# Two experts per token by sorting into blocks, in place of all four with a gate

## What is computed

```python
x = x + conv(_gn(x))                        # spike attention, 8 heads, values rounded to 0..4
t = _to_tokens(x)
t = t + attention(_ln_t(t))                 # causal, 6 heads of 32
t = t + ffn(_ln_t(t))
...
scores = jnp.einsum('bsd,de->bse', x, gate_w) + gate_b          # 4 experts
probs = jax.nn.softmax(scores, axis=-1)
topk_vals, topk_idx = jax.lax.top_k(probs, TOP_K)               # TOP_K = 2
mask = jnp.sum(jax.nn.one_hot(topk_idx, NUM_EXPERTS), axis=-2)
masked = probs * mask / (jnp.sum(probs * mask, axis=-1, keepdims=True) + 1e-09)
h = gelu(jnp.einsum('bsd,edh->ebsh', x, w1) + b1)               # 192 -> 768
y = jnp.einsum('ebsh,ehd->ebsd', h, w2) + b2                    # 768 -> 192
out = jnp.einsum('bse,ebsd->bsd', masked, y)
```

## Time and profile before

| | us |
|---|---|
| median of 3 runs | 1736.04 (1730.72 to 1737.88) |
| the profiled execution | 1726.64 |
| its span, first to last instruction | 1724.8 |
| PE busy | 1581.2 |
| DVE busy | 1211.1 |
| ACT busy | 932.3 |
| POOL busy | 234.4 |

### The profile page before, as it was taken

How to read it: one execution, slowest core, us unless ns; L and a number is a source line. 1 busy time by engine, 2 the same in 40 slices (tenths; PEclk the granted TensorE clock), 3 DMA queues, 4 the chain that set the end, 5 groups by cost and what they waited for, 6 DMA issues and landing times.

```text
span 1724.8 us, 32985 instructions
## 1 busy us (share of the span) xinstructions
PE 1581.2 (92%) x13264; PEld 1018.6 (59%) x13264; DVE 1211.1 (70%) x2544; ACT 932.3 (54%) x1378; POOL 234.4 (14%) x296
## 2 busy tenths in 40 slices
PE   1579999899999999999999999999999999999998
PEld 0334576556765566655765557654666556765666
DVE  6776875857867676767758587676776777686743
ACT  2315655366544765456553665537654566536664
POOL 3021112011020112001030110201111010301100
PEclk9668999999999999999999999999999999999999
DMA  4221002010020001010020100201001100200000
GB/s 128 97 55 38 1 1 65 1 48 1 1 65 29 20 1 46 20 48 1 2 65 1 47 2 1 65 1 47 1 22 45 47 2 2 64 2 11 1 10 10
DMA packets 25102, 48.19 MB, mean 28 GB/s; under 512 B 7411, under 2 KB 16819, under 8 KB 23573
## 3 DMA queue, kind: packets, MB, share of 16 engines
q1 hardware_dynamic: 15840, 28.63, 6.1%
q0 software_dynamic: 6144, 9.45, 2.3%
q10 hardware_dynamic: 2966, 8.01, 1.3%
HBM read 20.70 MB, written 6.29 MB: 16 GB/s over the span
## 4 chain that ended last, share of the span: by engine, by line
PE 64%; DVE 25%; ACT 5%; issue 3%; DMA 1%; POOL 1%; SPq 0%; DVEq 0%; ACTq 0%
PE ps L429 20%; PE ps L707 16%; PE ps L654 8%; DVE mx L1157 7%; PE ps L464 5%; PE ps L588 4%; DVE acc L1313 3%; DVE room L1329 3%; PE ps L508 2%; DVE u L1027 2%; PE ps L436 1%; DVE norm_stats L998 1%; PE ps L495 1%; ACT room L870 1%; DVE gn_st L1040 1%
## 5 line engine op out<-in xcount | busy, mean ns | idle before, releaser
L870 ACT ACTIVATE room<-ps,b_sb 128x512 f32<-128x512 f32 x384 | 263.2, 686 | 461.9 <-PE ps L429 460.7
L707 PE MATMUL ps<-wout_h,room 128*128 128x192 f16 x3072 | 462.4, 247 | 5.4 <-DVE acc L1313 5.4
L1329 DVE SCALAR_TENSOR_TENSOR room<-room 128x512 f16<-128x512 f32 x384 | 263.6, 690 | 177.8 <-ACT room L876 172.8
L707 PE MATMUL ps<-wout_l,room 128*128 128x192 f16 x1536 | 379.4, 247 | 0.0
L707 PEld LDWEIGHTS ps<-wout_h,room 128*128 128x128 f16 x3072 | 287.8, 98 | 46.0 <-DVE acc L1313 11.8
L848 ACT ACTIVATE room<-ps 128x1024 f32<-128x1024 f32 (+3 forms) x288 | 225.4, 809 | 143.1 <-PE ps L468 90.8
L1157 DVE TENSOR_REDUCE mx<-ps 128x2 f32<-128x1024 f32 (+3 forms) x288 | 266.3, 953 | 40.4 <-PE ps L592 19.9
L876 ACT ACTIVATE room<-room 128x512 f16<-128x512 f32 x384 | 241.9, 630 | 34.3 <-PE ps L707 0.7
L654 PE MATMUL ps<-room,v 128*64 128x512 f32 (+3 forms) x1152 | 232.6, 488 | 0.0
L588 PE MATMUL ps<-qk 96*128 96x512 f16 (+3 forms) x576 | 160.6, 352 | 37.6 <-DVE mx L1157 28.2
L464 PE MATMUL ps<-qk 98*64 98x512 f16 (+3 forms) x1152 | 157.2, 333 | 11.7 <-DVE mx L1157 7.8
(11 more groups left out here) (210 smaller groups left out, 2382.3 us busy)
## 6 DMA issues: line engine op xcount, KB each, us to landing
xc<-x_ch SPq DMA_DIRECT2D x8, 768.0 KB, 6.0
qk<-qk_all SPq DMA_DIRECT2D x96, 64.0 KB, 2.5
qk<-qk_all POOLq DMA_DIRECT2D x96, 64.0 KB, 2.5
out<-acc ACTq DMA_DIRECT2D x16, 384.0 KB, 2.5
xt<-x_tok SPq DMA_DIRECT2D x7, 768.0 KB, 7.3
qk<-qk_all POOLq DMA_DIRECT2D x96, 32.0 KB, 2.0
qk<-qk_all SPq DMA_DIRECT2D x96, 32.0 KB, 2.3
room<-w_in SPq DMA_DIRECT2D x2, 1024.0 KB, 10.6
```

What stands on the lines that cost most here:

```text
L707: mm = pe.matmul(dst, hid[:, s, tok], w[:, n, :], start=(k == 0 and m == 0 and t % 2 == 0), stop=False, skip_group_check=True)
L870: act.activation(h32[:, i % N_H, :], ps[:, H_BANK[i], :], ACT.Gelu, scale=1 / (U_SCALE * W_SCALE), bias=b1_sb[:, n:n + 1])\
L1329: V.scalar_tensor_tensor(out=h_l[:, s, :], in0=h32[:, s, :], scalar=A_SCALE, in1=h_h[:, s, :], op0=ALU.mult, op1=ALU.subtract)\
```

## The change

The experts work on blocks of 128 slots in place of chunks over all tokens. For each half of 512 tokens (1,024 pairs of token and expert) there are always 11 blocks: 8 full ones and 3 for the padding of four experts to whole blocks.

- `tail` routes: gate scores from float32 values, the chosen experts as a 0/1 tile `sel`, small matmuls with a triangle and with ones that count the earlier tokens of each expert, and on DVE a chain of small steps that gives each token its two slots (`slots_u`), the weights (`weight`), and a table of the expert that owns each block (`table`). `TAIL_STEPS` goes from 33 to 44. The high and low parts of a token are written as one row of 512 values (`rows16`, with two ones for b1).
- POOL writes the rows to DRAM by slot (`scatter`, eight indirect DMAs), SP reads each block back transposed into `o16` (`fetch`, four slots), PE loads the table into registers and addresses the weights of `hidden` and `expert_out` by them; b1 is part of the product (`win_b`), gelu has no bias. ACT copies a block's output from PSUM (`take`), SP stores it to DRAM (`keep`), POOL fetches each token's two rows (`gather`, eight indirect DMAs), and DVE adds them with their weights (`combine`, eight instructions), half 0 at step 41 of experts, half 1 in the next image's attend at item 17.
- The first part of `front` (group statistics, relu, spikes of x) becomes `early`; for images after the first it runs in the previous image's attend. Half 1's output projection moves from step 4 of 48 to step 11; block 0 is due at step 14.5 and then one block each 1.57 steps, with q, k and v projections of the next image (steps 10.5 to 14.5) ahead of it. `F_LAG` is 2 blocks, `N_H` 2.
- Setup stages b1 on two rows, converts it on DVE (`biases_ready`), copies part of `win_t` into `win_b` and clears the row buffers in DRAM; POOL has three more fills.

```diff
+TOP = 2
+HALF_BLOCKS = TOP * TB + EXPERTS - 1
+BLOCKS = NB * HALF_BLOCKS
+X_SLOTS = 4
...
+AFTER = 100
+EXPERTS_FROM, BLOCK_STEPS = 14.5, 1.57
+TAIL_AT = ({"wo": 20, "residual": 20, "norm": 24, "rows": 26, "turn": 27, "high": 28, "scores": 30,
+            "gate": 30, "best": 32, "route": 36, "place": 36},
+           {"wo": AFTER + 11, "residual": AFTER + 11, "norm": AFTER + 13.5, "rows": AFTER + 15,
+            "turn": AFTER + 16, "high": AFTER + 16.2, "scores": AFTER + 17.5, "gate": AFTER + 17.5,
+            "best": AFTER + 20, "route": AFTER + 21.5, "place": AFTER + 21.5})
...
+EARLY_AT = {"stats": 2, "sums": 5, "sums2": 7, "variance": 7.5, "clip": 10, "relu": 12, "xs": 14}
...
+            "high": 25, "low": 25, "qk": 26, "qk_lo": 26, "spread": 28, "v": 30, "maxima": 34.5}
+COMBINE_AT, COMBINE_LATER_AT = 41, 17
+SCORES_AT = (50, 51)
...
 PIECE_AT = (10, 12, 14, 16, 18, 20, 21.5)
-PER_CHUNK = 2.75
...
+        x_rows = [nc.dram_tensor(f"x_rows{b}", (HALF_BLOCKS * P, ROW), F16, kind="Internal").ap() for b in range(NB)]
+        y_rows = [nc.dram_tensor(f"y_rows{b}", (HALF_BLOCKS * P, C), F32, kind="Internal").ap() for b in range(NB)]
...
+            def fetch(img, n):
+                b, slot = n // HALF_BLOCKS, n % X_SLOTS
+                i = n % HALF_BLOCKS
+                if i == 0:
+                    sp.wait_ge(scattered[b], at(scattered[b], img, whole(scattered[b])))
+                if n >= X_SLOTS:
+                    sp.wait_ge(h_ps, at(h_ps, img, 2 * (n - X_SLOTS + 1)))
+                sp.dma_start_transpose(o16[:, :, slot * P:(slot + 1) * P], x_rows[b][i * P:(i + 1) * P, :])\
+                  .then_inc(x_in[slot], 16)
...
+            Aside(spread(0)).finish()
+            for img in range(B):
+                spread_maxima(img, 1)
+                if img + 1 < B:
+                    load_tokens(img + 1)
+                if img + 2 < B:
+                    load_channels(img + 2)
+                for n in range(X_SLOTS):
+                    fetch(img, n)
+                experts(img, Aside(spread(img + 1) if img + 1 < B else iter(())))
...
+                yield when["route"]
+                pe.wait_ge(sel_ready, at(sel_ready, img, b + 1))
+                earlier = TB * EXPERTS
+                pe.matmul(ps[:, 3, earlier:2 * earlier], tri16[:, :],
+                          sel[:, :, :].rearrange("p t e -> p (t e)"), start=True, stop=False,
+                          skip_group_check=True)
+                for t in range(1, TB + 1):
+                    dst = ps[:, 3, earlier + t * EXPERTS:earlier + (t + 1) * EXPERTS]
+                    for s in range(t):
+                        mm = pe.matmul(dst, ones16[:, :], sel[:, s, :], start=False,
+                                       stop=(t == TB and s == TB - 1), skip_group_check=True)
+                mm.then_inc(route_ps, 1)
...
+                def experts_of(b):
+                    pe.wait_ge(table_ready, at(table_ready, img, b + 1))
+                    return nc.values_load_multi_w_load_instructions(
+                        table[b][0:1, :], engines=PE_ONLY, min_val=0, max_val=EXPERTS - 1,
+                        skip_runtime_bounds_check_because="the table counts, of four starts of which "
+                        "the first is zero, those not after the block, less one: 0 to 3")[1]
...
+                    first = e * HID
+                    for m in range(HC):
+                        if n and m % TB == 0:
+                            pe.wait_ge(h_act, at(h_act, img, 2 * (n - 1) + 1 + m // TB))
+                        dst = ps[:, m // TB, m % TB * P:(m % TB + 1) * P]
+                        w_h = win_h[:, COL_W1 + m * P:][:, bass.ds(first, P)]
+                        w_l = win_l[:, COL_W1 + m * P:][:, bass.ds(first, P)]
+                        w_t = win_t[:, COL_W1 + m * P:][:, bass.ds(first, P)]
+                        w_b = win_b[:, m * P:][:, bass.ds(first, P)]
+                        for k, (w, c) in enumerate(((w_h, 0), (w_h, 2), (w_l, 0), (w_t, 1), (w_b, 3))):
+                            mm = pe.matmul(dst, w, o16[:, c, slot * P:(slot + 1) * P],
+                                           start=(k == 0), stop=(k == 4))
...
+                        pe.wait_ge(ut_done, at(ut_done, img, 2))
+                    else:
+                        pe.wait_ge(y_out, at(y_out, img, n if n <= HALF_BLOCKS else n - 1))
+                    pe.wait_ge(h_lo, at(h_lo, img, n + 1))
+                    first = e * (HC * C)
+                    for m in range(HC):
+                        hid = slice(m * P, (m + 1) * P)
+                        w_h = wout_h_flat[:, m * C:][:, bass.ds(first, C)]
+                        w_l = wout_l_flat[:, m * C:][:, bass.ds(first, C)]
+                        for k, (h, w) in enumerate(((h_h, w_h), (h_l, w_h), (h_h, w_l))):
+                            pe.matmul(dst, h[:, s, hid], w, start=(m == 0 and k == 0), stop=False)
+                    pe.matmul(dst, b2_ones[:, :], b2_sb[:, bass.ds(e * C, C)], start=False, stop=True)\
...
+                    elif n >= N_H:
+                        act.wait_ge(h_lo, at(h_lo, img, n - N_H + 1))
+                    for part, (bank, cols) in enumerate(((0, slice(0, QB)), (1, slice(QB, HID)))):
+                        act.wait_ge(h_ps, at(h_ps, img, 2 * n + part + 1))
+                        act.activation(h32[:, s, cols], ps[:, bank, 0:cols.stop - cols.start], ACT.Gelu,
...
+                def take(n):
+                    act.wait_ge(f2_done, at(f2_done, img, n + 1))
+                    if img or n >= 2:
+                        act.wait_ge(y_stored[n % 2], at(y_stored[n % 2], img, 16 * (n // 2)))
+                    act.activation(y_sb[:, n % 2, :], ps[:, y_bank(n), 0:C], ACT.Copy).then_inc(y_out, 1)
...
+            def scatter(img, b):
+                pool.wait_ge(slots_ready, at(slots_ready, img, b + 1))
+                pool.wait_ge(row_hi, at(row_hi, img, 2 * (b + 1)))
+                pool.wait_ge(row_lo, at(row_lo, img, b + 1))
...
+                for ab in range(TOP):
+                    for t in range(TB):
+                        i = ab * TB + t
+                        nc.gpsimd.indirect_dma_start(
+                            x_rows[b], bass.IndirectOffsetOnAxis(ap=slots_u[b][:, i:i + 1], axis=0),
+                            rows16[:, t, :], None).then_inc(scattered[b], 16)
+                pool.wait_ge(scattered[b], at(scattered[b], img, whole(scattered[b])))
+            def gather(img, b):
+                for s in range(2):
+                    done = len(range(s, HALF_BLOCKS * (b + 1), 2))
+                    pool.wait_ge(y_stored[s], at(y_stored[s], img, 16 * done))
+                if b:
+                    pool.wait_ge(combined, at(combined, img, 1))
+                elif img + 1 < B:
+                    pool.wait_ge(a_tr, at(a_tr, img + 1, NB))
...
+                for ab in range(TOP):
+                    for t in range(TB):
+                        i = ab * TB + t
+                        nc.gpsimd.indirect_dma_start(
+                            y_got[ab][t], None, y_rows[b],
+                            bass.IndirectOffsetOnAxis(ap=slots_u[b][:, i:i + 1], axis=0))\
+                          .then_inc(gathered[b], 16)
+                pool.wait_ge(gathered[b], at(gathered[b], img, whole(gathered[b])))
...
+            for img in range(B):
+                if img:
...
+                    low_of_output(img, run)
+                pool.wait_ge(o_lo, at(o_lo, img, PAIRS))
+                power_of_tail(img, 0)
+                low_of_output(img, PAIRS)
+                low_of_output(img, PAIRS + 1)
+                pool.wait_ge(o_lo, at(o_lo, img, PAIRS + 2))
+                scatter(img, 0)
+                low_of_output(img, PAIRS + 2)
+                pool.wait_ge(o_lo, at(o_lo, img, NB * PAIRS))
+                power_of_tail(img, 1)
                 gate_exp_of_block_1(img)
-            attend(B - 1)
...
+                    token_power(img + 1)
+                    pool.wait_ge(pow_done, at(pow_done, img + 1, 2))
+                else:
+                    pool.wait_ge(gate_exp, at(gate_exp, img, 2))
+                scatter(img, 1)
+                if img + 1 < B:
+                    spread_keys(img + 1)
+                gather(img, 0)
+            gather(B - 1, 1)
...
+                V.tensor_scalar(n_blocks[:, :], total, 1 / P, (P - 1) / (2 * P), ALU.mult, ALU.add)\
+                 .then_inc(tail_step, 1)
+                dve.wait_ge(tail_step, at(tail_step, img, steps.more(1)))
...
+                dve.wait_ge(tail_step, at(tail_step, img, steps.more(1)))
+                V.tensor_reduce(base[:, :], lower[:, :, :], AX.X, ALU.add).then_inc(tail_step, 1)
+                dve.wait_ge(tail_step, at(tail_step, img, steps.more(1)))
+                V.scalar_tensor_tensor(out=place[:, :, :], in0=base[:, None, :].broadcast_to(each), scalar=float(P),
```

(22 more changed lines are left out.)

747 lines of the change are left out of this document (450 added, 297 removed).

## The result

The changed kernel takes 2040.4 us (median of four runs, 2038.1 to 2045.2) against 1737.0 for the kernel before: the ratio is 1.176, 95% interval 1.172 to 1.180. The forecast was 1650, faster. The profiled execution has a span of 2036.3 us; the sum of the prediction had 1638.

What follows compares the result with a forecast made beforehand. PE was taken to bound the experts stage. Span 1724.8 - 98 (seven pairs of stages at -14) + 11 (start +8, last image +3) = 1638 us, 1650 in terms of the runs' median; range 1575 to 1800.

Steps and rivals of the forecast that it cites:

- It is bound by PE: Experts stage of the kernel before: PE's matmuls fill 143 of 155 us, 10 to 12 us are stalls.
- 17 us off: Experts stage with a front: 138 us against 155.2, of 24.6 us of expert matmul time saved an image.
- the 63 us of the first stretch: Front until the maxima, with 12.7 blocks: 63.0 us of PE's matmuls, taken as 66 for stalls.
- The second, 53 forecast: Maxima with the last 9.3 blocks: PE 47.2 us, DVE 46.9, both full, taken as 53 us.
- I take 65: Expert matmuls of 128 columns with register-addressed weights: 65 ns each, between 59 and 98; 77.4 us an image.
- Rival (b): Expert matmuls: register-addressed weight load not pulled ahead, 98 ns each, 21.8 us an image more, 1810 us; chance 0.13.
- rival (c): Expert matmuls: issuing a register load takes three slots, 75 to 81 ns a pair, +53 to +84, 1703 to 1734; chance 0.14.
- Part 2's chain: Routing of half 0 after attention: steps, scatters, landing and transposing load, 16 us (12 to 22); stretch before block 0, 17.
- Part 4: Attention stage: early moves in, +3 us (0 to 6); low_of_output behind scatter 0 needed only by block 1's tail.
- Part 5: The ends: start +8 us (4 to 15); last image's experts 117 us, +3, with unhidden routing and 17 at the end.
- (d): Feed of blocks: a transposing load over 5.5 us sets the pace; at 6.5 us each, 1825 us; chance 0.13.
- (a): Experts stage, all goes well: 59 ns matmuls, early stretch 12 us, DVE 97% full, 126 us; total 1560; chance 0.14.

Runs made afterwards that it cites:

- e14: The kernel before with two of the five 512-column matmuls of every hidden chunk left out (output not the reference's): 1673.1 us, ratio 0.967.
- e10: e9 with the register arithmetic of a chunk packed into two fused instructions ahead of its five matmuls: 1880.5 us, ratio 1.086.
- e11: e9 with three of the five matmuls of each hidden chunk and two of the four register instructions left out: 1862.8 us, ratio 1.075.
- e8: e7 with constant weight addresses in place of registers (output not the reference's): 1878.3 us, ratio 1.085.
- e7: e6 with the normalization of the next image's early part asked for six items later in attention: 1952.3 us, ratio 1.126.
- e9: e7 with the last pair's low part computed on DVE, so GpSimd's scatters of half 0 don't wait for it: 1939.2 us, ratio 1.120.
- e6: Changed kernel with the last pair's low part ahead of the scatters and block 1's normalization 2.7 steps later on DVE: 1988.8 us, ratio 1.147.
- e15: e10 with the next image's q matmuls issued ahead of block 1's output projection on PE: 1872.2 us, ratio 1.084.
- e2: Changed kernel with each weight address computed one chunk ahead, about as many register instructions: 2178 us, ratio 1.256.
- e3: Changed kernel with the last pair's low part ahead of the eight scatters in GpSimd's queue: 2162 us, ratio 1.244.
- e4: Changed kernel with the normalization of the next image's early part asked for six items later in attention: 2166 us, ratio 1.249.
- e16: e15 with DVE computing each block's low part one block later in its queue: 1943.6 us, ratio 1.124.
- e18: The kernel of e16 once more, on another chip: 1944.5 us, ratio 1.123.

## Why the prediction was wrong

**The step that failed first: "It is bound by PE", and with it "17 us off" of 24.6.** The prediction read 99% busy PE in one stretch and 10 to 12 us of stalls as a stage whose time is PE's sum. e14 tests just this exchange, in the kernel before: 20.7 us less give 5.9, and PE is idle for 10 us more. The recorded durations overlap (an L707 matmul lasts 247 ns and starts every 83, rows 3 and 4), so a busy PE is not one without room. The expert matmuls lie between the front's steps by a hand-written schedule, and shorter ones don't let the next front step start earlier where it waits for ACT or DVE; this last is argued from the waits that grew, as no run has another order of the front. I had raised the 63 us of the first stretch to 66 for this; it took 85 in the changed kernel. The second, 53 forecast with both engines full, took 67, with DVE busy for 45, 67% and not over 85%. With packed registers and another queue order (e10) blocks and rest are 145.7 us against 121: some 25 x 7 = 175 us, the largest term. e11 shows that little of it is PE's work. About 6 of the 25 us are the lower clock, by the estimate above, so 40 to 45 of the 175; the rest are waits.

**A granted clock of 1.00, taken over without a word.** The sum prices every matmul at 2.4 GHz. The changed kernel has 0.68 before block 0 and 0.94 and 0.95 in the two block stretches, behind idle time of PE.

**"I take 65".** The size was right for the median and wrong for the mean, by which the sum goes. The bounds were 59 to 98 ns, the mean 85 and 98 in the last image: the upper bound, from another mechanism than the weight load's 98 ns. The argument from the 4-column gate matmuls counted PE's issue slots for matmuls and forgot that a register address has to be computed: 24 register instructions among 30 matmuls. Rival (b)'s price was met (98 ns), its consequence not: 22 us an image came only in the last image (106.3 to 83.6 by e10); in the others 4.5 to 6, since waits take the rest. In all 59 us by e10, 74 by e8. That 59 lies within rival (c)'s 53 to 84 is luck: (c) has it as time of PE in all eight images. The Trainium skill's 81 ns at N=128 (page "TensorE: Matmul & The Clock Gate", section "Back-to-back issue gap") is not met by either: 56 ns with fixed and with packed addresses at 2.4 GHz, 95 to 98 on average with interleaved ones. The register loads are small, as forecast: eleven values last 1.3 us in the trace, twice an image.

**Part 2's chain, "16 us", stretch "17 us".** Steps by name, in e7: place chain 2.9 us (3 forecast), eight scatters 1.26 us apart, 10 us (I took 8), landing and transposing load 5.2 (5). So these terms hold to 2 us. Between the place chain and the scatters, the chain that ended last in e7 has 5.8 us more (the last normalization on DVE, the high part on ACT, the low part on GpSimd), for which the 16 us had nothing; the last image of e9, which has only this chain and DVE's last normalization, takes 18.7. What failed is Part 4's sentence on low_of_output behind scatter 0, "1 us of work needed only by block 1's tail": it is needed by block 1's projection, which stands in PE's queue ahead of q, k and v. e6 priced it at 7.0 us an image, 54 us in all; q, k and v, largely at the lower clock, are most of the rest, as e15 showed by taking 5.2 more.

**Part 4, "+3 us (0 to 6)".** Right once GpSimd is out of the way: 51.9 to 52.9 us in e7 to e10 against 51, and 50.6 where the clock is 1.00. In the changed kernel 57.7, as group_power waits behind the gathers of the image before, DVE behind it, and PE behind DVE: 37 us (e6 to e7). My text had gathers, queue and "early" in one paragraph and did not ask who needs GpSimd meanwhile. That it named 8 us of growth as the point at which it falls was right: it grew by 10.

**Part 5.** The start was +2.8 where I took 8. The last image: 30 us from the last hidden matmul to the end against 20 forecast (3 + 17), blocks 109 against 77, of which the registers 23. The trace has the 10 us at the end in three places. The last block's copy from PSUM ends 6.7 us after the last hidden matmul, where I took 3 for the drain. From the first gather to the landing of the last it is 11.4, where I took 8 + 2.5. From the last combine to the end of the span, with the store of the output, it is 7.1 us, 2.8 in the kernel before, and the sum had nothing for it.

**The rivals.** (d), the feed, is out: a transposing load lands after 2.7 us (median), and PE waits for one at block 0 only (e7: 18.7 us in seven waits, 10.3 of them in the last image, and none at a later block). (a) needed a PE-bound stage. (c)'s issue price existed, in the instructions that compute the address and not in the matmul. None of them was "the front's chains come to light", the largest single term; the prediction was near it, as it had put PE's stalls at 10 to 12 us of a stage while 102 us of filler stood ready to cover the chains.

Accounting for the 398 us of span: uncovered chains of the front, with the clock, 7 x 25 = 175; the stretch before block 0, 7 x 15 = 107; attention 7 x 6.7 = 47; registers 7 x 4.9 + 23 = 57; the rest of the last image 24; start -5: 405, read from different runs, each of them uncertain by some us. No variant of the change comes below the kernel before: the best that computes what it should, e15, is at 1.084. What the chains would need, another order of the front or more buffers between its steps, was not tried.

## What to carry to other kernels

Before you count on saved work of an in-order engine, ask what waits that work was covering: take the same amount out of the kernel as it is (e14 did it with one edit) and see how much comes back. For each slow block of instructions put on a helper engine (here 10 us of scatters, 10 of gathers) list every result that others need from it meanwhile, and what stands behind those in their queues. Where an address comes from a register, look at the instructions that compute it, pack them ahead of the matmuls, and judge by the mean of starts, not by the median. Where a change leaves an engine idle between its matmuls, price them at the clock that such stretches have in the trace.

## What the runs showed of the hardware

- Register arithmetic between matmuls of 128 columns: four instructions per five matmuls, 474 ns; two, 280 ns, the same as none. One before each matmul: 124 ns a start (e11). Computing ahead without packing changed nothing (94 ns in e2, 96 in e3 and e4).
- An indirect transfer of 128 rows holds GpSimd for 0.96 us, and the next starts 0.30 later, scatter and gather alike, against 0.54 for a fixed copy. From the start of the issue of the last of eight to its landing it is 2.4 us for a scatter and 2.6 for a gather. A transposing load of 128 rows of 1 KB lands after 2.7 us (median).
- PE stood idle on nothing that the profile names for 0.3 to 2.2 us at a time in three of the six groups (25 to 69 us a run inside the expert matmuls), with kernels that differ by a few instructions from ones that had 0 to 2 us, while the kernel before kept its time on each chip. Groups were all one or all the other, so it looks like the chip; e16 and e18, one kernel, had it on two chips, the changed kernel not on two others. No kernel was seen both ways, so chip and program are not told apart. The Trainium skill (page "Runtime: NRT & Kernel Launch", section "Instruction fetch mechanics") has the fetch of instructions hidden behind their issue. Late fetches would look like these gaps, but no run here shows what they are.
- After its wait of 15.6 us behind the scatters PE runs at 1.2 GHz: a q matmul takes 0.43 us, and the stretch has a granted clock of 0.68. The kernel before, without such a hole, held 1.00 in the attention and experts stages of rows 2.
